# A Macaron transformer block on one core: lower parts of the probabilities on GpSimd, single window loads, bands by tile, rotary sums out of the bank

## The reference, cut to what matters

```python
x = x + 0.5 * ffn(layernorm(x))      # x: 8 x 512 x 128
x = x + attn(layernorm(x))
x = x + 0.5 * ffn(layernorm(x))
# ffn: 8 experts, summed: (silu(x @ wg) * (x @ wu)) @ wd, hidden width 512
# attn: 16 heads of 8; interleaved rotary on q and k; q / sqrt(8)
rel = rel_emb[clip(key - query, -32, 32) + 32]
scores = q @ k.T + einsum(q, rel)    # then causal mask
attn = softmax(scores)
ctx = attn @ v + einsum(attn, rel)
out = ctx @ w_o.T
```

## Time and profile before

| | |
|---|---|
| median of 3 runs | 1346.1 us (1344.24 to 1347.66) |
| profiled execution | 1341.76 us, its span 1340.0 us |
| busy TensorE, VectorE, ScalarE, GpSimd | 1314.1, 1220.2, 1048.7, 1068.3 us |
| transfers | 225.02 MB, 168 GB/s over the span |
| granted clock of TensorE, mean | 0.996 |

### The profile page before, as it was taken

How to read it: one execution, slowest core, us unless ns; L and a number is a source line. 1 busy time by engine, 2 the same in 40 slices (tenths; PEclk the granted TensorE clock), 3 DMA queues, 4 the chain that set the end, 5 groups by cost and what they waited for, 6 DMA issues and landing times. The chain is left out here.

```text
span 1340.0 us, 28494 instructions
## 1 busy us (share of the span) xinstructions
PE 1314.1 (98%) x8334; PEld 1052.6 (79%) x8334; DVE 1220.2 (91%) x2609; ACT 1048.7 (78%) x2098; POOL 1068.3 (80%) x980
## 2 busy tenths in 40 slices
PE   8999999999999999999999999999999999999798
PEld 6888877777788777778887778777887788888586
DVE  6887989999999999999999999999999999999565
ACT  6765878888878888788888888878888888888354
POOL 6986978889787878798778878788877887878465
PEclk9999999999999999999999999999999999999899
DMA  6504799999899999999989999999999999998300
GB/s 188 162 1 132 139 183 203 185 205 206 179 201 174 196 176 182 207 183 197 188 158 221 184 189 181 173 234 170 192 183 164 226 188 178 180 193 144 60 1 8
DMA packets 719517, 225.02 MB, mean 168 GB/s; under 512 B 653441, under 2 KB 698881, under 8 KB 719361
## 3 DMA queue, kind: packets, MB, share of 16 engines
q1 hardware_dynamic: 562224, 180.84, 69.1%
q10 hardware_dynamic: 157136, 42.36, 17.5%
HBM read 60.95 MB, written 69.86 MB: 98 GB/s over the span
## 5 line engine op out<-in xcount | busy, mean ns | idle before, releaser
L1219 POOL TENSOR_TENSOR hid_lo<-hid,hid_hi 128x512 fp32r<-128x512 f32 x512 | 663.4, 1304 | 170.9 <-ACT hid_hi L927 125.9
L921 ACT ACTIVATE hid<-work 128x512 f32<-128x512 f32 x512 | 305.8, 602 | 112.7 <-PE work L788 96.0
L1053 DVE SCALAR_TENSOR_TENSOR hid<-hid,work 128x512 f32<-128x512 f32 x512 | 343.1, 678 | 46.3 <-ACT hid L921 45.8
L1059 DVE TENSOR_TENSOR hid<-hid,work 128x512 f32<-128x512 f32 x512 | 345.6, 679 | 24.1 <-PE work L727 21.7
L927 ACT CAST hid_hi<-hid 128x512 fp32r<-128x512 f32 x512 | 318.8, 627 | 60.5 <-DVE hid L1059 36.7
L1234 POOL TENSOR_TENSOR probs<-exps,probs 128x512 f16<-128x512 f32 (+1 forms) x288 | 305.1, 1064 | 65.7 <-ACT probs L979 64.0
L968 ACT ACTIVATE exps<-work,negmax_shifted 128x512 f32<-128x512 f32 (+2 forms) x320 | 188.4, 605 | 46.0 <-DVE negmax_shifted L1159 27.3
L1153 DVE TENSOR_REDUCE negmax<-work 128x1 f32<-128x384 f32 (+3 forms) x352 | 219.9, 631 | 0.9
L784 PE MATMUL work<-xt,wg 128*128 128x512 f32 x512 | 205.6, 402 | 4.0 <-DVE hid L1053 2.5
L725 PE MATMUL work<-xt,wu 128*128 128x512 f32 x512 | 204.5, 399 | 0.5 <-ACT g_s L955 0.2
L808 PE MATMUL acc<-hid_lo,wd 128*128 128x512 f32 x512 | 203.4, 400 | 1.1 <-POOL hid_lo L1219 0.9
(11 more groups left out here) (94 smaller groups left out, 1745.6 us busy)
## 6 DMA issues: line engine op xcount, KB each, us to landing
prob_window_scratch<-probs SPq DMA_DIRECT2D x384, 80.0 KB, 2.9
rel_win<-rel_window_scratch ACTq DMA_DIRECT2D x250, 96.0 KB, 3.6
q_scratch<-rope SPq DMA_DIRECT2D x16, 512.0 KB, 4.6
qq<-q_scratch ACTq DMA_DIRECT2D x32, 256.0 KB, 3.5
k_scratch<-rope SPq DMA_DIRECT2D x16, 512.0 KB, 4.2
rel_window_scratch<-g_s SPq DMA_DIRECT2D x32, 256.0 KB, 3.8
k_pad<-k_scratch SPq DMA_DIRECT2D x128, 64.0 KB, 3.6
prob_window_scratch<-probs SPq DMA_DIRECT2D x32, 256.0 KB, 3.8
```

The lines of the kernel that those rows point to most:

```text
L921: act.activation(hid[:, arg % HB, :], work[bank_of["gate", arg]][:, :], ACT.Tanh, scale=0.5).then_inc(s_tanh, 1)
L1053: dve.scalar_tensor_tensor(out=hid[:, arg % HB, :], in0=hid[:, arg % HB, :], scalar=1.0, in1=work[bank_of["gate", arg]][:, :], op0=ALU.add ...
L1059: dve.tensor_tensor(hid[:, arg % HB, :], hid[:, arg % HB, :], work[bank_of["up", arg]][:, :], ALU.mult).then_inc(s_hid, 1)
L1219: pool.tensor_tensor(hid_lo[:, arg % HH, :], hid[:, arg % HB, :], hid_hi[:, arg % HH, :].bitcast(F32), ALU.subtract).then_inc(s_hlo, 1)
```

## The change

The low parts of all probabilities are made by GpSimd out of the two SBUF buffers, and all maxima are shifted; the scores' bank comes free after the exponential. The window of a tile is one load of 128 rows and 160 columns. Bands are loaded tile by tile, four transfers a group. The product with the sine is written back into the projection's bank, and the sums read it there. The four transposes of a norm each wait for their own tile. In the last pass the last hid_lo is made by VectorE, and the copy, the transposes, the sum and the store go in two halves, the second through another bank. The planner's costs and all its offsets are other ones.

```diff
-    def lent(k):
-
-        return k % GK in (2, 3, 4, 5, 6, 7, 8, 9, 10)
...
-    BANDS = ((0, 1, 2), (3,))
+    BANDS = ((0,), (1,), (2,), (3,))
...
     def band_of(quad):
-        return quad // NT * len(BANDS) + (0, 0, 0, 1)[quad % NT]
+        return quad // NT * len(BANDS) + quad % NT
...
-             1133.0, "denominators": 54.7, "down": 35.1, "down_lo": 29.5, "exp": -173.7, "fill": 412.2, "gate": 23.6,
-             "gated": 71.3, "hi": -198.0, "largest": -162.3, "ln_hi": -529.1, "ln_lo": -689.7, "ln_rstd": 1093.6,
...
-             -463.4, "load_k": 142.9, "load_q": -750.4, "load_window": 12.7, "load_x": -324.4, "near": -107.3, "outproj":
...
-             "rotate": 1052.3, "scale": -1319.7, "scores": 8.4, "shift": -711.3, "split_hi": 141.7, "split_lo": -128.0,
...
+             1074.5, "denominators": 39.0, "down": 44.7, "down_lo": -94.3, "exp": -193.1, "fill": 521.1, "gate": -28.2,
+             "gated": 183.2, "hi": -86.6, "largest": -197.9, "ln_hi": -568.0, "ln_lo": -633.9, "ln_rstd": 1056.7,
...
+             "load_expert": -532.7, "load_k": 266.2, "load_q": -703.2, "load_window": -43.9, "load_x": -482.7, "near":
+             -272.8, "outproj": -281.5, "p_hi": -262.3, "p_lo": -1729.1, "p_turn": 105.6, "prepare_hi": -328.9,
...
+             "rotate": 1032.7, "scale": -1256.8, "scores": -95.7, "shift": -661.4, "split_hi": 54.6, "split_lo": -163.7,
...
-        step("POOL", 1.25, at + 3.7, "lo", n, ("hi", n), ("down_lo", back(n, HH)))
+        step("POOL" if n < NP * CH - 1 else "DVE", 1.25 if n < NP * CH - 1 else wide(L), at + 3.7, "lo", n, ("hi", n), ("down_lo", back(n, HH)))
...
-            step("DVE", wide(L) + w % 2 * 0.9, at, "rotate", (t, w), ("project", (t, w)))
+            step("DVE", wide(L) * (1 + w % 2), at, "rotate", (t, w), ("project", (t, w)))
...
-                step("ACT", 1.03, max(begin - 13, first - 13), "load_window", quad, ("qrel_store", gg),
+                step("ACT", 0.42, max(begin - 13, first - 13), "load_window", quad, ("qrel_store", gg),
...
-                 ("load_k", quad // NT), done_with(back(k, 2)))
+                 ("load_k", quad // NT), ("exp", back(k, 2)))
...
-            if lent(k):
-                step("DVE", 0.07 * HEADS[i], due[k] + 0.8, "shift", k, ("largest", k))
-            step("ACT", HEADS[i] * 0.07 + columns / 1200, due[k] + 1, "exp", k, ("shift" if lent(k) else "largest", k),
-                 ("p_lent", lent_before(k, EB) if lent(k) else None))
-            step("ACT", act_wide(columns) + 0.04 * lent(k), due[k] + 1.5, "p_hi", k, ("exp", k), ("store_band", back(k, PB)),
+            step("DVE", 0.09 * HEADS[i], due[k] + 0.8, "shift", k, ("largest", k))
+            step("ACT", HEADS[i] * 0.07 + columns / 1200, due[k] + 1, "exp", k, ("shift", k), ("p_lo", back(k, EB)))
+            step("ACT", act_wide(columns) + 0.04, due[k] + 1.5, "p_hi", k, ("exp", k), ("store_band", back(k, PB)),
...
-            if lent(k):
-                step("POOL", 0.04 + columns / 475, due[k] + 2, "p_lent", k, ("p_hi", k))
-            else:
-                step("DVE", wide(columns), due[k] + 2, "p_lo", k, ("p_hi", k))
-            step("SP", 1.5 if columns == L else 1.25, due[k] + 2, "p_turn", k, lower(k),
+            step("POOL", 0.04 + columns / 475, due[k] + 2, "p_lo", k, ("p_hi", k))
+            step("SP", 1.5 if columns == L else 1.25, due[k] + 2, "p_turn", k, ("p_lo", k),
...
-            return s_win[quad % WB], 16 + 32 * (quad // WB)
+            return s_win[quad % WB], 16 * (quad // WB + 1)
...
         def exp_of(k):
-            return exps[:, lents_to[k] % EB, :] if lent(k) else work[bank_of["scores", k]]
+            return exps[:, k % EB, :]
...
-                    sp.wait_ge(s_sum, PASS_OF["B", arg] + 1)
-                    sp.dma_start(out_v[arg], x_s[arg % XB][:, :].rearrange("p (t d) -> p t d", t=NT)
-                                 ).then_inc(s_out[arg % XB], 16)
+                    x = x_s[arg % XB][:, :].rearrange("p (t d) -> p t d", t=NT)
+                    halves = (slice(0, NT),) if arg < B - 1 else (slice(0, NT // 2), slice(NT // 2, NT))
+                    for h, half in enumerate(halves):
+                        sp.wait_ge(s_sum, PASS_OF["B", arg] + 1 + h)
+                        sp.dma_start(out_v[arg][:, half, :], x[:, half, :]).then_inc(s_out[arg % XB], 16)
...
+            def norm_turned(m, bank):
+                for i in range(NT):
+                    pe.wait_ge(s_xn, NT * m + i + 1)
+                    done = pe.transpose(bank[:, i * P:(i + 1) * P], xn[:, i * P:(i + 1) * P], ident[:, :])
+                done.then_inc(s_xnt, 1)
...
-                    if was == "scores" and not lent(x):
-                        pe.wait_ge(*lower_part(x))
-                    if was == "scores" and lent(x):
+                    if was == "scores":
                         quad, i, places, _ = task(x)
                         pe.wait_ge(s_exp, unit(quad, places[-1]) + 1)
...
                     if was == "project":
-                        pe.wait_ge(s_rope, rotated(*x))
+                        pe.wait_ge(s_rope, 6 * x[0] + (1, 3, 4, 6)[x[1]])
...
                 if name == "down_lo":
-                    pe.wait_ge(s_hlo, arg + 1)
+                    if arg < NP * CH - 1:
+                        pe.wait_ge(s_hlo, arg + 1)
+                    else:
+                        pe.wait_ge(s_hlo_last, 1)
...
-                    pe.wait_ge(s_acc, arg + 1)
-                    transposes(bank, acc_t).then_inc(s_ftok, 1)
+                    if arg < NP - 1:
+                        pe.wait_ge(s_acc, arg + 1)
+                        transposes(bank, acc_t).then_inc(s_ftok, 1)
+                    else:
+                        pe.wait_ge(s_hid, NP * CH)
+                        for i in range(NT):
+                            half = (bank, work[spare])[i // 2]
+                            if i % 2 == 0:
+                                pe.wait_ge(s_acc, arg + 1 + i // 2)
+                            done = pe.transpose(half[:, i * P:(i + 1) * P], acc_t[:, i * P:(i + 1) * P], ident[:, :])
+                            if i % 2 == 1:
+                                done.then_inc(s_ftok, 1)
...
-                    done = act.activation(xn[:, i * P:(i + 1) * P], x[:, i * P:(i + 1) * P], ACT.Identity,
-                                          scale=rstd[:, i:i + 1], bias=shift[:, i:i + 1])
-                done.then_inc(s_xn, 1)
+                    act.activation(xn[:, i * P:(i + 1) * P], x[:, i * P:(i + 1) * P], ACT.Identity,
+                                   scale=rstd[:, i:i + 1], bias=shift[:, i:i + 1]).then_inc(s_xn, 1)
...
-                    act.mul(acc_t[:, :], acc[:, :], 0.25).then_inc(s_acc, 1)
+                    if arg < NP - 1:
+                        act.mul(acc_t[:, :], acc[:, :], 0.25).then_inc(s_acc, 1)
+                    else:
+                        for half in (slice(0, L // 2), slice(L // 2, L)):
+                            act.mul(acc_t[:, half], acc[:, half], 0.25).then_inc(s_acc, 1)
...
-                    act.wait_ge(s_max, arg + 1)
                     scores = work[bank_of["scores", arg]]
-                    if lent(arg):
-
-                        wait(act, s_plent, lents[arg] - EB)
-                        act.wait_ge(s_shifted, lents[arg])
+                    act.wait_ge(s_shifted, arg + 1)
+                    wait(act, s_plo, arg + 1 - EB)
...
-                        bias = shifted[:, place:place + 1] if lent(arg) else negmax[:, place:place + 1]
                         act.activation(exp_of(arg)[:, n * keys:(n + 1) * keys], scores[:, n * keys:(n + 1) * keys], ACT.Exp,
-                                       scale=-1.0, bias=bias).then_inc(s_exp, 1)
+                                       scale=-1.0, bias=shifted[:, place:place + 1]).then_inc(s_exp, 1)
...
-                    if lent(arg):
-                        act.mul(probs[:, arg % PB, 0:cols], exp_of(arg)[:, 0:cols], 1.0).then_inc(s_phi, 1)
-                    else:
-                        act.mul(probs[:, arg % PB, 0:cols], exp_of(arg)[:, 0:cols], SCALE).then_inc(s_phi, 1)
+                    act.mul(probs[:, arg % PB, 0:cols], exp_of(arg)[:, 0:cols], 1.0).then_inc(s_phi, 1)
...
-                    halves = ((0, P, 0, W),) if arg < WB else ((0, P // 2, 0, P // 2 + R), (P // 2, P, P // 2, W))
-                    for top, end, left, right in halves:
-                        act.dma_start(rel_win[top:end, arg % WB, left:right, :].rearrange("p c a -> p (c a)"),
-                                      bass.AP(zwin_t, gg % 2 * NQ * TILE + i * HQ * W + top * NQ * W + left * HQ,
-                                              [[NQ * W, end - top], [1, (right - left) * HQ]])
-                                      ).then_inc(s_win[arg % WB], 16)
+                    act.dma_start(rel_win[:, arg % WB, :, :].rearrange("p c a -> p (c a)"),
+                                  bass.AP(zwin_t, gg % 2 * NQ * TILE + i * HQ * W, [[NQ * W, P], [1, HQ * W]])
```

(40 more changed lines are left out.)

60 lines of the change are left out of this document (21 added, 39 removed).

## The result

The changed kernel takes 1371.2 us, median of 4 runs (1359.59 to 1374.63); the kernel before, on the same chip, 1345.45 (1344.24 to 1347.66). The ratio is 1.0181, interval 1.0148 to 1.0214: slower by 1.8%, some 25 us. I had forecast 1335.6, with 1353 as the upper end. The profiled execution of the changed kernel took 1374.63 us, 32.9 more than that of before; its mean granted clock is 0.986 where before had 0.996.

The account below looks back on a forecast made before the run. TensorE, busy 98%, was taken as the bound, so only its idle places could win: ends -2.5, middle -4, hole -4, together -10.5 from 1341.76 to 1331.3 profiled; with 4.3 for the runs' median, 1335.6 us, range 1322 to 1353.

Parts of the forecast that it names:

- the window bytes: Window loads: 320 KB in one load against 192 in two, 16 MB more in all, costed at nothing.
- The far bound of 87 us: Window loads: price of the 16 MB at the middle's 188 GB/s if the cover of early requests is gone.
- my rival's tenth: Rival that window bytes bind: a tenth of the far bound, +9 - 2.5, giving 1352.6 us; chance 0.07.
- ScalarE's issues: ScalarE's queue: 125 window issues fewer (-77), 64 band loads more (+24), net -53 us, half taken as gain.
- VectorE and GpSimd: Engine loads: VectorE -25.8 us, GpSimd +75.0; in the middle, waits for VectorE and ScalarE -6, for GpSimd +2.
- the first rival: Only the ends come: reordering leaves the hole, middle waits change owner; -2.5, 1343.6 us; chance 0.20.
- the stock of the middle: Weight loads' waits between 150 and 1250 us, 20.8 us in all, taken as everything the middle can win.
- GpSimd as the bound: Rival: exponentials wait on lower parts queued behind hid_lo; +10, less 2.5, 1353.6 us; chance 0.13.
- The hole: TensorE idle 8.0 us before the last pass, plus 2.2 of lower clock; forecast to lose 4 of 10.2.
- the rival had it that I gave 0.15: Rival that the hole closes, for it the offsets: -2.5 - 10.2 and -8 in the middle, 1325.4 us; chance 0.15.
- The ends: Start -0.8 and last norm -0.8 from transposes tile by tile, halved tail -0.9: together -2.5 us.
- Rotary sums: 16 sums on VectorE lose their second SBUF input: -9.6 us, the product written into the bank taken as unchanged.

Follow-up runs that it names:

- the keys' run: Changed kernel with the 128 loads of the keys issued on ScalarE's queue in place of SyncE's, planned anew: 1378.09 us, ratio 1.0207.
- the one with two queues: Changed kernel with windows in two 96 KB halves, the upper issued on ScalarE's queue, the lower on SyncE's: 1338.55 us, ratio 0.9943.
- the narrow kernel: Changed kernel with each window from the fourth on as one load of 128 rows by the left 96 columns, 192 KB: 1337.14 us, ratio 0.9931.
- The run with the offsets of before: Changed kernel planned with the offsets of the kernel before, the planner's costs staying the new ones: 1369.46 us, ratio 1.0181.
- the narrow load: Kernel before with each window as one load of 128 rows and the left 96 columns, 192 KB: 1337.54 us, ratio 0.9941.

## Why the prediction was wrong

**The step that failed** is the one on the window bytes: "I cost this at nothing". They cost 34 us in the changed kernel, nearly the whole error (1371.2 - 1335.6 = 35.6). Its reason was that a 320 KB load landed in 3.4 us and the 96 KB ones in 3.6, "the transfers don't queue deeply, and windows are asked for well ahead". By the medians that still holds after the change, and it doesn't decide. First, a median says nothing on the few transfers that land late: the turns' median stayed at 3.9 us while their longest went from 7.7 to 12.5, and the windows' longest went from 7.7 to 11.9. Second, I asked who waits for the windows, and nobody does. I should have asked who waits for what shares the engines with them: p_hi, with four buffers, waits for every turn. How much of the 34 us passes through the turns is open, as the keys' run and the one with two queues show. The DMA share of 1.00 in the middle was a sign to heed, though not a ceiling: after the change it is 1.02, at 200 GB/s instead of 188. The far bound of 87 us was right to carry; at four tenths of it, my rival's tenth was too small, and its chance of 0.07 far too small. My test for it, window loads landing after 5 us, would have missed it as well: they land in 4.0.

**ScalarE's issues.** I took half of 53 us off ScalarE's queue and gave it a part of -6. One load fewer a window is worth -10 to -13 us in the changed kernel and -8 in that of before, so the term was right in sign and too small. The loads that are left are also quicker to issue, 0.338 us at the median instead of 0.617, so by the sum's own working their issues fell from 156 us to 43 (128 x 0.338), by more than its 77. The row at 711.85 was a weak witness: it names VectorE's near as what ended ScalarE's 1.48 us. On SyncE's queue, planned, the second load costs the changed kernel nothing.

**VectorE and GpSimd.** The busy times came as forecast; the gain from them did not, and this is the second step that failed. The waits of the weight loads changed owner, as the first rival had it. In the narrow kernel those for VectorE fall from 19.7 to 11.9 us (all rows of the view of the earlier trace rows), but those for exponentials rise from 5.6 to 8.8 and those for hid_lo from 2.1 to 8.0. In the kernel before with all lower parts on GpSimd the three are 12.2, 18.8 and 3.5, and its time is even. In the changed and in the narrow kernel ScalarE's exponentials wait some 16 us for GpSimd's lower parts, and before it was 1.7. The sum had +2 for GpSimd and nothing for this. It also took 20.8 us of waits of the weight loads as the stock of the middle, where TensorE itself was idle for 7.3. The sentence of the Trainium skill's Perfetto Trace Analysis (Optimizing Scalar/DVE Operations) on moving work between these two, which I carried as a rival, gives the right time; the run doesn't show its reason, since VectorE's busy time did fall by 28 us. GpSimd as the bound, at 0.13, is not what made the change slower, but the waits that it foresaw are part of what the middle lost.

**The hole** lost all of its 8 us, not 4, in the changed kernel and in its narrow variant. The sum's reason was VectorE's relief. The run with the offsets of before, where VectorE is relieved as much, keeps 5.65 us of it, so the new offsets closed most of it, as the rival had it that I gave 0.15. The middle of the narrow kernel stands for more (14.1 us against 7.3) instead of less:

```profile
150.00:1250.00 1100.00, 1085.90 (x7330) 865.51 (x7330) 1021.63 (x2427) 910.81 (x1826) 959.48 (x885) 1.00 0.98 188
1250.00:1290.00 40.00, 40.00 (x186) 33.17 (x185) 27.61 (x50) 23.41 (x44) 25.79 (x23) 1.00 0.03 7
```

That 1337.1 lies near the forecast is thus luck: the middle lost 7 us where it should have won 4, and the hole gave all it had. The kernel before gets to 1337.54 with the narrow load and nothing else of the change.

**The ends** came near the sum, -3 us (uncertain by some 2) where it had -2.5, but not in all their pieces. The start and the tail after the change, answering to the earlier trace rows:

```profile
7.15 1.54 PE L705 MATMUL work<-ident,xn 128*128 128x128 f32 x4 [0.24 <-ACT xn L889]
...
9.45 0.77 PE L755 MATMUL work<-xt,wg 128*128 128x512 f32 x1 [0.77 <-ACT xt L896]
```
```profile
1366.49 0.73 DVE L1073 TENSOR_TENSOR hid_lo<-hid,hid_hi 128x512 fp32r<-128x512 f32 x1 [0.69 <-ACT hid_hi L909]
...
1367.34 0.61 PE L782 MATMUL acc<-hid_lo,wd 128*128 128x512 f32 x2
...
1368.52 0.63 PE L795 MATMUL work<-ident,xn 128*128 128x128 f32 x4 [0.56 <-ACT xn L923]
1368.97 0.76 DVE L1082 TENSOR_TENSOR x<-work,x 128x256 f32<-128x256 f32 x2 [1.74 <-PE work L795]
```

The transposes end at 8.69 instead of 9.53, the 0.8 of the sum, and the first gate starts at 9.45 (10.29 before). From the end of the last matmul to the end of the span it is 4.85 us, and it was 4.98: of the tail the halving gave 0.1, not 0.6. The last hid_lo is ready at 1367.22, ahead of the last two matmuls, so the 0.24 of waiting is gone. **Rotary sums** fell by 647 and 484 ns each, 9.0 us of VectorE where 9.6 was forecast, and the product with the sine takes 696 ns, and 682 before; alone they were not tried. **Bands by tile** at nothing: still without a price.

## What to carry to other kernels

Where the transfer engines read a share near 1.00 and the issuing queues are busy, added bytes and added issues can have a price even if nobody waits for them: look past the median landing time, at what waits for the transfers that share the engines, and don't forecast nothing. In these kernels the price of the bytes was two to four tenths of the upper bound. Before relieving a busy engine, ask who will be waited for next. A merged load that trades an issue for bytes is two edits, and is to be timed as both. An experiment that adds traffic also adds issues and rows; without the run that adds these alone, its result is read for more than it shows.

## What the runs showed that I had not expected

- Copies of 2 KB, 125 of them, which land in 3.0 us and which nothing waits for, cost 27 us; 126 KB more in each cost another 15. At the middle's 188 GB/s the 16 MB would be 87.
- Turns of the same median behave differently: at 3.8 and 3.9 us to landing they held others for 9.0 us (narrow windows) and 28.9 (full ones). The issue stretches as well: 1.25 us at the median, 4.82 at the longest, 3.78 in the chain shown; before the change it was 1.24 and 3.55.
- One load of 320 KB beats two of 160 KB by 13 us, but two of 96 KB, which carry less, beat it by 23.
- Another set of the planner's offsets, with nothing else changed, opened or closed the hole ahead of the last pass (5.65 us or none) and left the time of the whole as it was.
